# Gate and up products of a feed-forward block as seven block products, in units of 256 tokens

## The reference

```python
routed = sigmoid(x @ w_router + b_router) > 0.5
v = rmsnorm(x, norm1_w) @ wv + bv
h = x + v @ wo
h2 = rmsnorm(h, norm2_w)
mlp = (silu(h2 @ w_gate) * (h2 @ w_up)) @ w_down    # 512 -> 1408 -> 512
ffn = where(routed, h + mlp, x)
```

## Time and profile before

| | us |
|---|---|
| median of three runs | 4421.18 |
| lowest and highest | 4418.03, 4424.27 |
| profiled execution | 4421.92 |
| its span in the trace | 4420.1 |
| first gate product | 66.04 |
| last down product over (about) | 1142.3 |

### The profile page before, as it was taken

How to read it: one execution, slowest core, us unless ns; L and a number is a source line. 1 busy time by engine, 2 the same in 40 slices (tenths; PEclk the granted TensorE clock), 3 DMA queues, 4 the chain that set the end, 5 groups by cost and what they waited for, 6 DMA issues and landing times.

```text
span 4420.1 us, 77500 instructions
## 1 busy us (share of the span) xinstructions
PE 4348.0 (98%) x28720; PEld 2987.7 (68%) x28720; DVE 2558.0 (58%) x5514; ACT 2348.6 (53%) x5915; POOL 1306.0 (30%) x1414
## 2 busy tenths in 40 slices
PE   8999999999899999999999999999999999999998
PEld 4444444444577777777777777777777777777776
DVE  4322222220366666666767776666667776676674
ACT  1111111110366666666666766666666676676675
POOL 1000000000123333333333333334344334443344
PEclk9999999999999999999999999999999999999999
DMA  4000000000200000000000011011111111111111
GB/s 142 30 26 24 30 11 30 28 14 25 93 20 21 23 21 23 21 21 28 23 21 21 25 40 61 23 54 35 42 35 45 35 37 37 35 44 37 35 35 42
DMA packets 108759, 154.13 MB, mean 35 GB/s; under 512 B 31841, under 2 KB 49249, under 8 KB 108385
## 3 DMA queue, kind: packets, MB, share of 16 engines
q1 hardware_dynamic: 72288, 93.94, 6.3%
q10 hardware_dynamic: 36096, 55.24, 4.0%
HBM read 113.73 MB, written 35.42 MB: 34 GB/s over the span
## 4 chain that ended last, share of the span: by engine, by line
PE 69%; DVE 1%; ACT 1%; POOL 1%; issue 1%; POOLq 0%; ACTq 0%; DVEq 0%
PE bank L958 20%; PE bank L1255 10%; PE bank L962 10%; PE bank L1532 10%; PE bank L1440 3%; PE bank L1426 2%; PE bank L1466 2%; PE bank L1401 2%; PE bank L1378 2%; PE bank L1154 1%; PE bank L1091 1%; PE bank L1155 1%; PE bank L1517 1%; PE bank L1007 1%; PE bank L1048 1%
## 5 line engine op out<-in xcount | busy, mean ns | idle before, releaser
L958 PE MATMUL bank<-xtile,wt 128*128 128x259 f32 x4096 | 1095.3, 394 | 21.1 <-DVE vraw L988 15.8
L958 PEld LDWEIGHTS bank<-xtile,wt 128*128 128x128 f32 x4096 | 723.0, 192 | 142.5 <-DVE vraw L988 45.4
L1312 ACT ACTIVATE xyinv<-bank 128x512 f16<-128x512 f32 x768 | 453.3, 593 | 276.4 <-PE bank L1255 273.6
L1532 PE MATMUL bank<-wot,xnt 128*128 128x512 f32 x1024 | 542.8, 620 | 0.8 <-ACT xnt L1525 0.8
L962 PE MATMUL bank<-wt,xtile 128*128 128x512 f32 x1024 | 524.5, 615 | 0.0
L1288 DVE TENSOR_TENSOR wlev<-bank,mask 128x256 f16<-128x256 f32 x768 | 317.1, 419 | 294.0 <-PE bank L1255 289.2
L988 DVE SCALAR_TENSOR_TENSOR vraw<-bank,taps,vraw 128x256 f32<-128x256 f32 x768 | 368.8, 480 | 62.2 <-ACT vraw L981 44.2
L1221 POOL TENSOR_TENSOR ltl<-ltm,lth 128x512 f16<-128x512 f32 x128 | 149.2, 1166 | 766.0 <-ACT lth L1215 766.0
L435 DVE TENSOR_TENSOR hid<-bank,gate 128x512 f32<-128x512 f32 x88 | 60.9, 692 | 490.2 <-PE bank L417 490.2
L1207 POOL TENSOR_TENSOR ltm<-ltm,mask 128x512 f32<-128x512 f32 x128 | 159.1, 1243 | 604.8 <-DVE ltm L1195 604.8
L412 PE MATMUL bank<-h2t,wt 128*128 128x512 f32 x704 | 325.4, 606 | 0.8 <-DVE h2t L387 0.8
(11 more groups left out here) (180 smaller groups left out, 8635.5 us busy)
## 6 DMA issues: line engine op xcount, KB each, us to landing
grows<-row_scratch ACTq DMA_DIRECT2D x126, 256.0 KB, 3.2
xtile<-xt_scratch ACTq DMA_DIRECT2D x30, 518.0 KB, 3.8
xn<-x SPq DMA_DIRECT2D x32, 256.0 KB, 5.5
xt_scratch<-xt SPq DMA_DIRECT2D x8, 1024.0 KB, 5.8
g_scratch<-sel SPq DMA_DIRECT2D x32, 256.0 KB, 2.0
part_scratch<-prow SPq DMA_DIRECT2D x32, 256.0 KB, 2.0
prow<-part_scratch SPq DMA_DIRECT2D x32, 256.0 KB, 2.6
sel<-g_scratch SPq DMA_DIRECT2D x32, 256.0 KB, 2.9
```

The costliest lines, as they stand in the source:

```text
L958: j = pe.matmul(b_p[:, 0:WIN], wt[:, k, c:c + P], xtile[:, par, k, :], **st)
L1312: act.activation(dst, b_inv[p][:].rearrange("p (a h b s) -> p a h b s", a=2, h=HEADS, s=z), ACT.Copy).then_inc(s[f"xy_sb{p}"], 1)
L1532: i = pe.matmul(b_o[:], xnt[:, h], wot[:, h], start=(h == 0), stop=(h == GV - 1))
```

## The change

A unit is 256 tokens, two blocks of 128, so there are 16 units. For one hidden tile of 128 features and a unit, gate and up are one 2x2 block product: the rows are (gate, up) times the two halves of the 512 inputs, the columns are the two token blocks. It is taken by Strassen's scheme in Winograd's form: seven block products instead of eight, each of two f32 products of 128 columns (`quarter`).

The weights' combinations `s1` to `s4` are made once by DVE (`dve_combine`, in two parts, 768 and 640 of the 1408 features; `s4` takes the place of `a21`, the other three lie in `comb`). The tokens' combinations `T1`, `T2`, `T3`, `N4` are made by POOL for each unit (`pool_tokens`, four instructions of 256 elements). Four of the seven products go to the four quarters of bank 2 or 3 (`pe_gate`), three to bank 4 or 5 (`pe_rest`), one tile later in the order. The results are put together in `part`, which has three buffers: ACT copies the first quarter (`act_first`), DVE adds in two instructions (`dve_sums`, 128 and 256 elements) and, after the rest, in two more (`dve_outs`, 128 and 384), ACT takes the Silu of 256 elements and POOL multiplies (`pool_hidden`).

Also: `front` is written anew for two blocks, with a gate step between the two "columns"; POOL walks the common list now, its layer norm step in two parts; `pe_down` waits for the hidden tiles one by one; the gate and up weights come in two parts, and the merged-weight operands are staged in `comb` and no longer in `hid`; SP's wait ahead of `w_qkvz` is on the last rest product. Some semaphores are joined.

```diff
-FTILE = 512
+FTILE = 256
...
-        h2t = sb("h2t", [P, 2, KT, FTILE])
-        gate = sb("gate", [P, 2, FTILE])
+        KH, FIRST = KT // 2, 6 * P
+        B11, B12, B21, B22, T3, T2, N4 = range(7)
+        T1 = B12
+        hb = sb("hb", [P, 2, N4 + 1, KH, P])
+        part = sb("part", [P, 3, 4, P])
         hid = sb("hid", [P, FT, FTILE])
-        wvt_sb, wo_sb = hid[:, 0:KT, :], hid[:, KT:2 * KT, :]
+        comb = sb("comb", [P, 3, KH, FF])
+        a11, a12, a21, a22 = wg_sb[:, 0:KH], wg_sb[:, KH:KT], wu_sb[:, 0:KH], wu_sb[:, KH:KT]
+        s1, s2, s3, s4 = comb[:, 0], comb[:, 1], comb[:, 2], a21
+        staged = comb[:].rearrange("p s k f -> p (s k f)")
+        wvt_sb, wo_sb = (staged[:, i * KT * D:(i + 1) * KT * D].rearrange("p (k d) -> p k d", k=KT) for i in range(2))
         sel = r["sel"]
...
-                dve.wait_ge(s["u_ps"], FT * (u - 1))
-            dve.tensor_tensor(h2t[:, u % 2, :, j * P:(j + 1) * P], bank[1][:].rearrange("p (k c) -> p k c", k=KT),
-                              n2_sb[:].unsqueeze(2).broadcast_to([P, KT, P]), ALU.mult).then_inc(s["h2td"], 1)
+                dve.wait_ge(s["gb_ps"], FT * (u - 1))
+            dve.tensor_tensor(hb[:, u % 2, j:B22 + 1:2], bank[1][:].rearrange("p (h k c) -> p h k c", h=2, k=KH),
+                              n2_sb[:].rearrange("p (h k) -> p h k", h=2).unsqueeze(3).broadcast_to([P, 2, KH, P]), ALU.mult).then_inc(s["h2td"], 1)
+
+        def pool_tokens(pool, u):
+
+            b = hb[:, u % 2]
+            pool.wait_ge(s["h2td"], NJ * (u + 1))
+            pool.tensor_tensor(b[:, T3], b[:, B22], b[:, B12], ALU.subtract).then_inc(s["tok"], 1)
+            pool.wait_ge(s["tok"], 4 * u + 1)
+            pool.tensor_tensor(b[:, T1], b[:, B12], b[:, B11], ALU.subtract).then_inc(s["tok"], 1)
+            pool.wait_ge(s["tok"], 4 * u + 2)
+            pool.tensor_tensor(b[:, T2], b[:, B22], b[:, T1], ALU.subtract).then_inc(s["tok"], 1)
+            pool.wait_ge(s["tok"], 4 * u + 3)
+            pool.tensor_tensor(b[:, N4], b[:, B21], b[:, T2], ALU.subtract).then_inc(s["tok"], 1)
...
-        def pe_gate_up(pe, u, f):
+        def dve_combine(dve, half):
+
+            f = slice(0, FIRST) if half == 0 else slice(FIRST, FF)
+            dve.wait_ge(s["g_in"], 32 * (half + 1))
+            dve.wait_ge(s["cb_ps"], 1)
+            dve.tensor_tensor(s1[:, :, f], a21[:, :, f], a22[:, :, f], ALU.add).then_inc(s["comb"], 1)
+            dve.tensor_tensor(s3[:, :, f], a11[:, :, f], a21[:, :, f], ALU.subtract).then_inc(s["comb"], 1)
+            dve.wait_ge(s["comb"], 4 * half + 2)
+            dve.tensor_tensor(s2[:, :, f], s1[:, :, f], a11[:, :, f], ALU.subtract).then_inc(s["comb"], 1)
+            dve.wait_ge(s["comb"], 4 * half + 3)
+            dve.tensor_tensor(s4[:, :, f], a12[:, :, f], s2[:, :, f], ALU.subtract).then_inc(s["comb"], 1)
+
+        def quarter(pe, dst, w, f, b, first):
+
+            for k in range(KH):
+                i = pe.matmul(dst, w[:, k, f * P:(f + 1) * P], b[:, k], start=first and k == 0, stop=k == KH - 1, skip_group_check=True)
+            return i
+
+        def pe_gate(pe, u, f):
+
+            n, b, acc = FT * u + f, hb[:, u % 2], bank[2 + (FT * u + f) % 2]
+            if f == 0:
+                pe.wait_ge(s["tok"], 4 * (u + 1))
+            if u == 0 and f * P in (0, FIRST):
+                pe.wait_ge(s["comb"], 4 if f == 0 else 8)
+            if n >= 2:
+                pe.wait_ge(s["sum_sb"], 2 * (n - 1))
+            quarter(pe, acc[:, 0:P], a11, f, b[:, B11], True)
+            quarter(pe, acc[:, P:2 * P], s2, f, b[:, T2], False)
+            quarter(pe, acc[:, 2 * P:3 * P], s1, f, b[:, T1], False)
+            quarter(pe, acc[:, 3 * P:4 * P], a22, f, b[:, N4], False).then_inc(s["ga_ps"], 1)
+
+        def pe_rest(pe, u, f):
+
+            n, b, acc = FT * u + f, hb[:, u % 2], bank[4 + (FT * u + f) % 2]
+            if n >= 2:
+                pe.wait_ge(s["out_sb"], 2 * (n - 1))
+            quarter(pe, acc[:, 0:P], a12, f, b[:, B21], True)
+            quarter(pe, acc[:, P:2 * P], s4, f, b[:, B22], False)
+            quarter(pe, acc[:, 2 * P:3 * P], s3, f, b[:, T3], False).then_inc(s["gb_ps"], 1)
...
+        def act_first(act, u, f):
             n = FT * u + f
...
-            for k in range(KT):
-                i = pe.matmul(bank[2 + f % 2][:], wg_sb[:, k, f * P:(f + 1) * P], h2t[:, u % 2, k, :], start=(k == 0), stop=(k == KT - 1))
...
-                pe.wait_ge(s["hid_sb"], n - 1 if f >= 2 else FT * u)
-            for k in range(KT):
-                i = pe.matmul(bank[4 + f % 2][:], wu_sb[:, k, f * P:(f + 1) * P], h2t[:, u % 2, k, :], start=(k == 0), stop=(k == KT - 1))
...
+            act.wait_ge(s["ga_ps"], n + 1)
+            if n >= 3:
+                act.wait_ge(s["hid_sb"], n - 2)
+            act.activation(part[:, n % 3, 0], bank[2 + n % 2][:, 0:P], ACT.Copy).then_inc(s["p1_sb"], 1)
...
+        def dve_sums(dve, u, f):
+
+            n = FT * u + f
+            p, acc = part[:, n % 3], bank[2 + n % 2]
+            dve.wait_ge(s["p1_sb"], n + 1)
+            dve.tensor_tensor(p[:, 3], acc[:, P:2 * P], p[:, 0], ALU.add).then_inc(s["sum_sb"], 1)
+            dve.wait_ge(s["sum_sb"], 2 * n + 1)
+            dve.tensor_tensor(p[:, 1:3], acc[:, 2 * P:].rearrange("p (a c) -> p a c", a=2), p[:, 3].unsqueeze(1).broadcast_to([P, 2, P]), ALU.add).then_inc(s["sum_sb"], 1)
+
+        def dve_outs(dve, u, f):
+
+            n = FT * u + f
+            p, acc = part[:, n % 3], bank[4 + n % 2]
+            dve.wait_ge(s["gb_ps"], n + 1)
+            dve.wait_ge(s["sum_sb"], 2 * n + 2)
+            dve.tensor_tensor(p[:, 3], acc[:, 2 * P:3 * P], p[:, 1], ALU.add).then_inc(s["out_sb"], 1)
+            dve.wait_ge(s["out_sb"], 2 * n + 1)
+            dve.tensor_tensor(p[:, 0:3], acc[:, 0:3 * P].rearrange("p (a c) -> p a c", a=3), p[:, 0:3], ALU.add).then_inc(s["out_sb"], 1)
...
         def act_gate(act, u, f):
             n = FT * u + f
...
+            act.wait_ge(s["out_sb"], 2 * n + 2)
+            act.activation(part[:, n % 3, 0:2], part[:, n % 3, 0:2], ACT.Silu).then_inc(s["g_act"], 1)
+
+        def pool_hidden(pool, u, f):
             n = FT * u + f
...
+            pool.wait_ge(s["g_act"], n + 1)
+            pool.wait_ge(s["out_sb"], 2 * n + 2)
             if u and f == 0:
-                dve.wait_ge(s["d_ps"], NJ * u)
-            dve.tensor_tensor(hid[:, f, :], bank[4 + f % 2][:], gate[:, f % 2, :], ALU.mult).then_inc(s["hid_sb"], 1)
+                pool.wait_ge(s["d_ps"], NJ * u)
+            pool.tensor_tensor(hid[:, f, :].rearrange("p (t c) -> p t c", t=2), part[:, n % 3, 0:2], part[:, n % 3, 2:4], ALU.mult).then_inc(s["hid_sb"], 1)
...
-                pe.wait_ge(s["hid_sb"], FT * (u + 1))
             for f in range(FT):
+                if j == 0:
+                    pe.wait_ge(s["hid_sb"], FT * u + f + 1)
                 i = pe.matmul(bank[6 + j % 2][:], hid[:, f, j * P:(j + 1) * P], wd_sb[:, f, :], start=(f == 0), stop=(f == FT - 1))
...
-        front = ["gate", "gate", ("columns", 0), ("columns", 1), "gate", ("attn", 0), ("scale", 0), ("columns", 2), "gate", "gate", ("back", 0), ("attn", 1), ("scale", 1),
-                 ("columns", 3), "gate", ("ba",), "gate", ("soft", 0), ("back", 1), ("attn", 2), ("scale", 2), "gate", ("soft", 1), "gate", ("soft", 2), ("back", 2), ("attn", 3), ("scale", 3),
-                 "gate", ("soft", 3), "gate", ("cum",), ("back", 3)]
+        front = ["gate", "gate", ("columns", 0), "gate", ("columns", 1), "gate", ("attn", 0), "gate", ("scale", 0), ("ba",), ("attn", 1), "gate", ("scale", 1), ("soft", 0),
+                 "gate", ("back", 0), ("soft", 1), "gate", ("soft", 2), ("back", 1), ("tokens",), "gate", ("soft", 3), "gate", "gate", ("cum",)]
         assert front.count("gate") == FT
...
                 elif step == "gate" and u:
+                    if u == 1 and f * P == FIRST // 2:
+                        order.append((("combine", 1), 0))
                     order.append((("gate", f), u - 1))
+                    if f:
+                        order.append((("rest", f - 1), u - 1))
                     f += 1
+            if u:
+                order.append((("rest", FT - 1), u - 1))
             order += merged([(("down", j), u - 1) for j in range(NJ)] if u else [], [(step, u + 1) for step in opening] if u + 1 < UNITS_F else [])
+            if u == 0:
+                order.append((("combine", 0), 0))
...
+                sp.wait_ge(s["x_in1"], 16)
+                for f in (slice(0, FIRST), slice(FIRST, FF)):
+                    sp.dma_start(wg_sb[:, :, f], kp(w_gate)[:, :, f]).then_inc(s["g_in"], 16)
+                    sp.dma_start(wu_sb[:, :, f], kp(w_up)[:, :, f]).then_inc(s["g_in"], 16)
+                    if f.start == 0:
+                        load(1)
+                sp.wait_ge(s["g_in"], 64)
```

(53 more changed lines are left out.)

42 lines of the change are left out of this document (13 added, 29 removed).

## The result

| | before | after |
|---|---|---|
| median of five runs, us | 4422.95 | 4402.43 |
| lowest and highest | 4418.03, 4424.27 | 4402.36, 4402.47 |
| profiled execution; its span | 4421.92; 4420.1 | 4402.47; 4400.5 |
| first gate product | 66.04 | 65.05 |
| last down product over | 1142.3 | 1124.1 |

After to before is 0.9955, 95% interval 0.9941 to 0.997: faster by 0.45%, about 20 us. The forecast was 4375 us. The time lies within the range, but less than half of the expected 46.6 us came. The lines of `quarter` are now 439, of sums 477 and 479, of outs 487 and 489, of the hidden product on POOL 502, of the token sums 403 to 409.

What follows compares the result with a forecast made beforehand. PE's product order was taken to bound the first stage: opening 62.6, clock 2.4, products 548.5, down 302.2, fronts 15 x 11.4, wait 9, sum 1095.7 against 1142.3; 46.6 us less gave 4375 us, range 4356 to 4408.

Steps and rivals of the forecast that it cites:

- Pace of a 128-column record: PE's gate and rest products: 0.1113 us per record, 548.5 us in all against 604.3 before, 55.8 less.
- the first rival: Records at pace 0.1088 and DVE in time: 12 and 9 us less, 4354 (4350 to 4364); chance 0.15.
- Down: PE's down products: same products per token, 302.2 us in the sum; the last ones no longer wait 0.88.
- Clock: PE's first products lose 2.4 us at half clock, which stays; the loss behind the run of line 476 goes.
- The 3.5 us that the prediction put down to shorter losses: First stage before: the unnamed rest of 10.2 us, put down to shorter clock losses and taken as gone.
- Second stage: After the last down product: code unchanged, its weights' loading still covered, so it starts as before.
- First gate product: End of the opening: 23.9 + 23.5 + 6.5 + 7.0 + handovers 1.7 = 62.6 us, against 66.0 before.
- the wait ahead of tile 10: In each front PE's tile 10 waits for sums 8 from DVE: 0.6 us, 15 times, 9 us.
- The 10.6 us of DVE's walk: DVE's queue in a front, sums 6 starting near 30.2 through sums 8: 10.6 us, ending at 40.8.
- The end of the stage: Last down product over: 62.6 + 2.4 + 548.5 + 302.2 + 15 x 11.4 + 9 = 1095.7 against 1142.3.
- DVE late: Rival: DVE slower ahead of sums 8, 4405 (4390 to 4415), or 4393 by POOL's products; chance 0.24.
- The other form, DVE 19% slower throughout: Form of DVE late: 2.0 us more wait in each of 15 fronts, and elsewhere in the front; 4405.

Runs made afterwards that it cites:

- small_pool: The changed kernel, but POOL's hidden product and token sums work on 8 of 256 elements, all instructions and waits kept; 4378.52 us, 0.9899 of before.
- spread_front: The changed kernel, whole, with ba, soft and back steps placed otherwise among the gate steps of the front; 4362.71 us, 0.9871 of before.

## Why the prediction was wrong in size

Point by point, forecast against the trace of after.

- Pace of a 128-column record: 0.1113 forecast, 0.1114 measured; a tile is 3.12. Right, and the faster pace of the first rival did not come. The Trainium skill, page "TensorE: Matmul & The Clock Gate", section "Back-to-back issue gap", had a larger gap at 128 columns; this trace, with 0.1114, does not show it.
- Down: 18.88 forecast, 18.89 measured. The last downs wait for nothing. Right.
- Clock: the first products lose 2.0 us against 2.4, and behind "ba" (line 544, 152.55 to 154.26) nothing is lost, and so behind the 14 others. Right. The 3.5 us that the prediction put down to shorter losses are there in the trace of before: the clock was 0.85 and 0.72 in the two windows of 4 us from 532, and 0.57 in the one from 944, each time behind line 476, 3.4 us in all. Of the kernel after, the window at that run and the one behind it, with the clock third from the right:

```profile
152.00:156.00 4.00, 4.00 (x27) 3.10 (x26) 1.68 (x5) 0.42 (x1) 0.88 (x2) 1.00 0.00 0
156.00:160.00 4.00, 4.00 (x25) 2.98 (x24) 0.75 (x1) 0.96 (x3) 0.25 (x2) 1.00 0.00 0
```

- Second stage 3276.4 against 3277.8: covered, as said.
- First gate product: 62.6 forecast, 65.05 measured. Four combinations take 7.0, as said (1.76 each). But the token sums fell beside the DVE instructions of unit 0's back 1 and soft 3 and made the four of them 1.94 us longer than in small_pool (0.75, 0.22, 0.22 and 0.23). The term had no place for that. The whole miss is 2.45; the 0.5 left was not traced, and the runs differ by as much in when this stretch starts (line 421 at 43.98 here, at 44.60 in small_pool). DVE in order of time, kernel after:

```profile
43.98 1.09 DVE L421 SCALAR_TENSOR_TENSOR h<-h,routed,xn 128x512 f32<-128x512 f32 x1
44.99 0.74 DVE L579 SCALAR_TENSOR_TENSOR xtile<-xtile 128x64 f32<-128x64 f32 x1
45.77 0.73 DVE L580 TENSOR_SCALAR xtile<-xtile 128x64 f32<-128x64 f32 x1
46.53 0.80 DVE L581 SCALAR_TENSOR_TENSOR xtile<-xtile 128x64 f32<-128x64 f32 x1
...
57.89 1.76 DVE L429 TENSOR_TENSOR comb<-wt 128x1536 f32<-128x1536 f32 x1
```

- **The failed term** is the wait ahead of tile 10, 0.6 us in each of 15 fronts, the 9 of the sum; it measured 1.95 in each, 29 in all. Its two ends were right on the PE side (tile 9's gate part and tile 8's rest over at 40.2 after the unit's start; measured 174.28 - 133.96 = 40.3) and at DVE's start (sums 6 at 30.2; measured 164.27 - 133.96 = 30.3). The 10.6 us of DVE's walk between sums 6 and sums 8 are 11.9 in the trace, and the 1.3 between them are the three stretched instructions above. The step at fault is that durations measured where POOL was idle were put into a stretch where the change itself starts POOL instructions. Each DVE length in the sum is right for a quiet POOL; small_pool shows it with a wait of 0.49 by the view (0.65 counted like the 1.95) for the 0.6.
- Behind the stop: a unit has some 0.36 more that the sum had at nothing. Four records behind the stop take 0.55 for 0.45; the last rest part starts 0.27 after line 602 for 0.11 in spread_front, since outs 8 are late by the same cause, and its first eight records take 1.00 for 0.90. So a unit is 66.91 for 65.2. Without all of it the front takes 64.62 - 34.3 - 18.9 = 11.4, which is the forecast's figure.

The end of the stage was forecast at 1095.7 and is 1124.1, 28.4 later: 2.45 opening - 0.4 clock + 15 x 1.72 = 25.8 for the units + 0.6 pace and rounding. The profiled time is 27.2 above the forecast for it, with 1.4 back from the second stage.

The rival "DVE late" was the right one, in the form with POOL as the cause. It named 1.2 us in this stretch by way of two whole POOL products; the trace has 1.30, from three stretches of which none is a whole product, so that the two figures lie so close is partly luck. It priced this at 4393; the opening's share and the 0.36 per unit make the rest. The other form, DVE 19% slower throughout, gave 4405, nearer to the time, but that was luck: what no POOL instruction met ran at its forecast length. The mechanism is the one that the Trainium skill, page "SBUF — State Buffer", section "Who interferes with whom", gives, and the trace agrees in which instructions grew. What spoke for the rival in the prediction was weaker than what I had: DVE's walk ended 0.6 after PE's, so any stretching there costs its full length 15 times, and the change's diff puts 11 + 4 POOL instructions per unit beside it. The chance of 0.24 was too low for that.

## What to carry to other kernels

When a change gives work to POOL, go through the DVE instructions that stand ahead of the next wait and price each that reads SBUF twice, or is a `tensor_scalar` on SBUF, as it runs beside POOL (in this stretch 0.34 to 0.54 us more for each line that collided). Do it first where the walk of the feeding engine ends within a microsecond of the one it feeds. The repair need not remove the collision: put one step of the bottleneck engine's work between the steps that collide, so that the late result is no longer the one waited for; here this gave 40 us (34 of them in the units, 4.4 in the opening), and choosing what stands ahead of the first product in the opening gave 6 more.
